# Feed-forward tail of a Mamba-2 block: low-rank part folded into the weight, 1/sigma applied behind the matmul, layer norm begun a step earlier

## What is computed

```python
x = layernorm(x + mixer(x))            # x: 2 x 512 tokens x 512
# mixer: in_proj, causal conv (4 taps), silu, chunked state-space scan over 128 heads
#   (8 groups, chunks of 128 tokens), y * silu(gate), RMS norm per group of 1024 channels, out_proj
h   = einsum('bsd,nrd->nbsr', x, lora_A)              # 8 adapters of rank 16: 128 rows
out = x @ W.T + bias + einsum('nbsr,nor->bso', h, lora_B * (2 * lora_weights))
x = layernorm(x + out)
```

## Time and profile before

| | us |
|---|---|
| median of 3 runs | 1672.47 (1672.35 to 1673.64) |
| profiled execution, whole | 1674.88 |
| its span, first to last instruction | 1673.1 |
| PE busy | 1618.5 (97%) |
| PEld busy | 1294.7 (77%) |
| DVE busy | 1346.7 (80%) |
| ACT busy | 1225.1 (73%) |
| POOL busy | 1026.7 (61%) |
| from 1571.0 (step 2 of the last unit) to the norm_sum behind the last project_out, 1646.2 | 75.2 |
| from there to the last product, 1667.5 | 21.3 |
| from there to the end | 5.6 |

### The profile page before, as it was taken

How to read it: one execution, slowest core, us unless ns; L and a number is a source line. 1 busy time by engine, 2 the same in 40 slices (tenths; PEclk the granted TensorE clock), 3 DMA queues, 4 the chain that set the end, 5 groups by cost and what they waited for, 6 DMA issues and landing times. The chain is left out here.

```text
span 1673.1 us, 26984 instructions
## 1 busy us (share of the span) xinstructions
PE 1618.5 (97%) x9072; PEld 1294.7 (77%) x9072; DVE 1346.7 (80%) x1855; ACT 1225.1 (73%) x2375; POOL 1026.7 (61%) x829
## 2 busy tenths in 40 slices
PE   7799999999999999999999999999999999999898
PEld 6577887778878788787887788777887778877665
DVE  5487798869988699787988689886998779787776
ACT  5777778777768867777877777787677778677742
POOL 4365756565676656666666666656566666666654
PEclk9899999999999999999999999999999999999999
DMA  3655444544454434544444544544444343434511
GB/s 123 195 129 99 117 95 113 110 105 99 96 143 97 114 84 97 128 100 119 79 121 111 105 104 91 136 96 110 95 90 146 94 124 80 106 114 96 134 32 45
DMA packets 236889, 178.67 MB, mean 107 GB/s; under 512 B 16464, under 2 KB 198736, under 8 KB 236368
## 3 DMA queue, kind: packets, MB, share of 16 engines
q1 hardware_dynamic: 235312, 175.72, 43.3%
q10 hardware_dynamic: 1440, 1.22, 0.2%
HBM read 172.17 MB, written 4.72 MB: 106 GB/s over the span
## 5 line engine op out<-in xcount | busy, mean ns | idle before, releaser
L948 POOL TENSOR_TENSOR w_lo<-raw,w_hi 128x512 fp32r<-128x512 f32 x209 | 292.1, 1398 | 309.2 <-ACT w_hi L709 308.1
L494 PE MATMUL proj<-x_hi,w_hi 128*128 128x512 f32 x1160 | 464.3, 400 | 14.7 <-DVE x_lo L1212 6.9
L495 PE MATMUL proj<-x_lo,w_hi 128*128 128x512 f32 x1160 | 454.2, 392 | 0.0
L496 PE MATMUL proj<-x_hi,w_lo 128*128 128x512 f32 x1160 | 453.8, 391 | 0.0
L1099 DVE SCALAR_TENSOR_TENSOR hs<-proj,uch,hs 128x511 f32<-128x511 f32 (+2 forms) x384 | 285.3, 744 | 64.8 <-ACT hs L736 59.6
L791 ACT ACTIVATE decay<-decay,tok 128x128 f32<-128x128 f32 x1024 | 312.4, 391 | 4.8 <-DMA decay<-acum_d 4.8
L1121 DVE TENSOR_TENSOR decay<-decay,cb 128x1024 f32<-128x1024 f32 x128 | 186.8, 1459 | 101.7 <-ACT decay L797 99.1
L1000 POOL TENSOR_TENSOR dh<-dh,eac 128x512 f32<-128x512 f32 x96 | 130.7, 1362 | 222.7 <-DVE eac L1147 222.7
L494 PEld LDWEIGHTS proj<-x_hi,w_hi 128*128 128x128 f32 x1160 | 219.7, 189 | 58.2 <-issue 13.6
L496 PEld LDWEIGHTS proj<-x_hi,w_lo 128*128 128x128 f32 x1160 | 219.1, 189 | 46.2
L495 PEld LDWEIGHTS proj<-x_lo,w_hi 128*128 128x128 f32 x1160 | 219.8, 189 | 41.8
(11 more groups left out here) (121 smaller groups left out, 2762.2 us busy)
## 6 DMA issues: line engine op xcount, KB each, us to landing
decay<-acum_d SPq DMA_DIRECT2D x128, 512.0 KB, 8.9
raw<-w_t SPq DMA_DIRECT2D x209, 256.0 KB, 6.2
eac<-eacum_d SPq DMA_DIRECT2D x192, 128.0 KB, 8.7
wo_raw<-wo_t SPq DMA_DIRECT2D x32, 256.0 KB, 8.6
c_new<-wo_t SPq DMA_DIRECT2D x32, 256.0 KB, 8.2
hs<-x_t SPq DMA_DIRECT2D x8, 256.0 KB, 5.6
acc<-x_tok SPq DMA_DIRECT2D x1, 2048.0 KB, 8.4
out<-acc SPq DMA_DIRECT2D x8, 256.0 KB, 2.0
```

Of the source, the lines that this page charges most:

```text
L494: nc.tensor.matmul(dst[:], w_hi[:, ws, k, :], x_hi[:, k, cols], start=(k == 0), stop=False)
L495: nc.tensor.matmul(dst[:], w_hi[:, ws, k, :], x_lo[:, k, cols], start=False, stop=False)
L496: mm = nc.tensor.matmul(dst[:], w_lo[:, ws, k, :], x_hi[:, k, cols], start=False, stop=(k == KC - 1))
L948: nc.gpsimd.tensor_tensor(w_lo[:, s].rearrange("p a b -> p (a b)"), raw[:, s, :], w_hi[:, s].rearrange("p a b -> p (a b)").bitcast(F32), A ...
```

## The change

- SP issues the five feed-forward loads at the end of unit 0 (step 7), without the wait for gated. lora_a is laid out 128 x 512, not transposed.
- The low-rank part is folded into the weight once: for each of the four k-slices fold_lora(k) computes A_k^T B on TensorE and adds the identity to its k-th 128 columns (the residual), and fold_weight(k) adds this to the weight on VectorE. B is scaled at the end of step 1; folds 0 and 1 stand in step 2 between yoff and p_yd, folds 2 and 3 at its end; VectorE's first two additions stand before g_lo of step 2, the others at its end.
- lora_down, copy_lora, the product with B and add_bias are gone. ffn is four products.
- ScalarE only centres the chunk (centre). The product of the centred chunk is multiplied by 1/sigma, and the bias added, by one three-operand instruction (add_ffn).
- norm_sum, take_var, inv_rms, add_normed and the first layer norm of chunk t are in step t + 1, at the end of each engine's step; scale_off stands behind take_var and add_out.
- The feed-forward steps are by a table: FFN_AT = {3: (0,), 4: (1, 2), 5: (3,), 6: (4,)}, the sums and the second norm SUM_AT = {4: (0,), 5: (1, 2), 6: (3,)}; the rest is behind the loop. The products take banks proj[1] and proj[2] in turn; turn(7) uses p_hid.
- The second norm is one ScalarE pass with scale and shift (shift_of, GpSimd); the last chunk's is on VectorE.

The diff, cut to its core:

```diff
-        FFN_BANK = lambda t: proj[1][:] if t < CPB or t % 2 == 0 else p_st[:]
+        FFN_BANK = lambda t: proj[1 + t % 2][:]
+        TURN_BANK = lambda t: p_hid[:].rearrange("p a b -> p (a b)") if t == CHUNKS - 1 else proj[0][:]
...
-                        if last and (e, c) == (1, 1):
-                            sp.wait_ge(gated, step(GROUPS - 1, 1, 0))
+                        if last and (e, c) == (0, 7):
...
+            def fold_lora(k):
+                if k == 0:
+                    pe.wait_ge(ffn_loaded, 80)
+                    pe.wait_ge(coef_ready, 1)
...
+                wait(pe, w_folded, k - 1)
+                nc.tensor.matmul(FFN_BANK(k), lora_a_sb[:, k * P:(k + 1) * P], lora_b_sb, start=True, stop=False)
+                nc.tensor.matmul(FFN_BANK(k)[:, k * P:(k + 1) * P], ident[:], ident[:], start=False, stop=True).then_inc(lora_ready, 1)
+            def turn(t):
+                pe.wait_ge(centred, t + 1)
+                if t < CHUNKS - 1:
+                    wait(pe, yt_copied, t)
...
+            def ffn(t):
+                pe.wait_ge(w_folded, KC)
+                wait(pe, ffn_sum, t - 1)
+                pe.wait_ge(yt_copied, t + 1)
                 for k in range(KC):
+                    mm = nc.tensor.matmul(FFN_BANK(t), yT(t)[:, k, :], ffn_w_sb[:, k, :], start=(k == 0), stop=(k == KC - 1))
+                mm.then_inc(ffn_out, 1)
...
+                        if ffn_step and c == 2:
+                            fold_lora(0)
+                            fold_lora(1)
...
-                        if ffn_step and c >= 4:
-                            ffn(c - 4)
-                        if ffn_step and c >= 3:
-                            turn(c - 3)
+                        if ffn_step and c in FFN_AT:
+                            turn(FFN_AT[c][0])
+                        if ffn_step and c == 7:
+                            turn(5)
...
                             project_out(g, e, c - 1)
+                            if ffn_step:
+                                norm_sum(g, c - 1, True)
...
+                        if ffn_step and c == 2:
+                            fold_lora(2)
+                            fold_lora(3)
+                        if ffn_step and c in FFN_AT:
+                            for t in FFN_AT[c][1:]:
+                                turn(t)
+                            for t in FFN_AT[c]:
+                                ffn(t)
...
             project_out(G, 1, 7)
             norm_sum(G, 7, True)
+            ffn(5)
             turn(6)
             turn(7)
             ffn(6)
             ffn(7)
...
+                            for t in FFN_AT.get(c, ()):
+                                copy_turned(t)
+                            if c == 7:
+                                copy_turned(5)
+                            for t in SUM_AT.get(c, ()):
+                                normalize(t)
+                            if c >= 1:
+                                centre(c - 1)
...
+            copy_turned(6)
+            centre(7)
+            copy_turned(7)
+            for t in range(4, CHUNKS - 1):
+                normalize(t)
...
+                            for t in SUM_AT.get(c, ()):
+                                rstd_of(1, t)
+                                shift_of(t)
+                            if c >= 1:
+                                inv_rms(g, c - 1)
+                                rstd_of(0, c - 1)
...
             def add_ffn(t):
-                dve.wait_ge(biased, t + 1)
                 dve.wait_ge(ffn_out, t + 1)
-                nc.vector.tensor_tensor(acc[:, t, :], acc[:, t, :], FFN_BANK(t), ALU.add).then_inc(ffn_sum, 1)
+                dve.wait_ge(ln_rstd[0], t + 1)
+                nc.vector.scalar_tensor_tensor(out=acc[:, t, :], in0=FFN_BANK(t), scalar=rstd[:, 0, t:t + 1], in1=bias_sb,
+                                               op0=ALU.mult, op1=ALU.add).then_inc(ffn_sum, 1)
+            def fold_weight(k):
+                dve.wait_ge(lora_ready, k + 1)
+                nc.vector.tensor_tensor(ffn_w_sb[:, k, :], ffn_w_sb[:, k, :], FFN_BANK(k), ALU.add).then_inc(w_folded, 1)
...
+                        if ffn_step and c == 2:
+                            fold_weight(0)
+                            fold_weight(1)
                         dve.wait_ge(ghi_ready, s + 1)
...
+                        if ffn_step and c == 7:
+                            take_var(g, 6)
+                            add_out(g, 6)
+                        if ffn_step:
+                            for t in SUM_AT.get(c, ()):
+                                add_ffn(t)
+                                ln_begin(1, t)
...
+                        if ffn_step and 0 < c < 7:
+                            take_var(g, c - 1)
+                        if e == 1 and c > 0 and not (ffn_step and c == 7):
                             add_out(g, c - 1)
...
+                        if ffn_step and c < 7 and (c + 1) % CPB:
+                            scale_off(g, e, c + 1)
+                        if ffn_step and c > 0:
+                            add_normed(g, c - 1)
+                            ln_begin(0, c - 1)
...
+                        if ffn_step and c == 1:
+                            dve.wait_ge(ffn_loaded, 80)
+                            nc.vector.tensor_scalar(lora_b_sb, lora_b_sb, lw[:], 2.0, ALU.mult, ALU.mult).then_inc(coef_ready, 1)
+                        if ffn_step and c == 2:
+                            fold_weight(2)
+                            fold_weight(3)
```

More of the change, by code:

```diff
@@ L473, in _ @@
             for t in range(CHUNKS):
-                sp.wait_ge(ln_done[1], t + 1)
+                if t < CHUNKS - 1:
+                    sp.wait_ge(normed, t + 1)
+                else:
+                    sp.wait_ge(last_normed, 1)
                 sp.dma_start(out[t], acc[:, t, :]).then_inc(stored, 16)
@@ L544, in project_out, with norm_sum @@
                 mm.then_inc(out_ready, 1)
-            def norm_sum(g, c, last):
+            def norm_sum(g, c, last=False):
                 pe.wait_ge(sqs_ready, step(g, 1, c) + 1)
@@ L643, in body @@
                             front(0, 0, 0)
-                        if e == 1 and c > 1:
-                            norm_sum(g, c - 2, last)
+                        if ffn_step and c == 2:
+                            fold_lora(0)
+                            fold_lora(1)
+                        if e == 1 and c > 1 and not last:
+                            norm_sum(g, c - 2)
                         elif e == 0 and c < 2 and not (g == 0):
-                            norm_sum(g - 1, 6 + c, False)
+                            norm_sum(g - 1, 6 + c)
                         pe.wait_ge(xdt_ready, s + 1)
@@ L675, in body @@
                             project_out(g, e, c - 1)
-                            if last and (e, c) == (1, 7):
-                                norm_sum(g, 6, True)
+                            if ffn_step:
+                                norm_sum(g, c - 1, True)
                         elif e:
@@ L689, in _ @@
             norm_sum(G, 7, True)
-            turn(5)
-            ffn(4)
-            lora_down(5)
+            ffn(5)
             turn(6)
-            ffn(5)
-            lora_down(6)
             turn(7)
             ffn(6)
-            lora_down(7)
             ffn(7)
@@ L936, in _ @@
             groups(body)
-            for t in range(5, CHUNKS):
-                copy_turned(t)
-                copy_lora(t)
+            copy_turned(6)
[3 more added lines that the diff above has]
+                normalize(t)
         @block.gpsimd
@@ L1050, in lagged_rms @@
             def lagged_rms(g, e, c):
-                if e == 1 and c > 1:
+                if e == 1 and c > 1 and g < G:
                     inv_rms(g, c - 2)
@@ L1059, in rstd_of, with shift_of @@
                 pool.wait_ge(ln_stats[w], t + 1)
[L1060 to L1074 removed]
+                nc.gpsimd.tensor_tensor(rstd[:, w, t:t + 1], var_eps[:, w, t:t + 1], minus_half[:], ALU.pow).then_inc(ln_rstd[w], 1)
+            def shift_of(t):
+                pool.wait_ge(ln_rstd[1], t + 1)
+                nc.gpsimd.tensor_tensor(shift[:, t:t + 1], minus_mean[:, 1, t:t + 1], rstd[:, 1, t:t + 1], ALU.mult).then_inc(shift_ready, 1)
+            groups(body)
             inv_rms(G, 7)
             rstd_of(0, 7)
[L1077 to L1082 removed]
+            for t in range(4, CHUNKS - 1):
+                rstd_of(1, t)
+                shift_of(t)
+            rstd_of(1, CHUNKS - 1)
         @block.vector
@@ L1251, in body @@
                             tap(g, tiles[0], 0, 3)
-                        if e == 1 and c == 7:
+                        if e == 1 and c == 7 and not last:
                             take_var(g, 5)
@@ L1262, in body @@
                         nc.vector.tensor_tensor(y[:], p_yd[:], dh[:], ALU.add).then_inc(y_ready, 1)
-                        if e == 1 and 1 < c < 7:
```

(1 more changed line is left out.)

154 lines of the change are left out of this document (36 added, 118 removed).

## The result

The changed kernel takes 1684.46 us (median of four, 1683.29 to 1686.17) where the kernel before takes 1672.80: 1.0061 times as long, 95% interval 1.0049 to 1.0074 (the two medians alone give 1.0070). A second comparison (e8) gave 1.0049 (1.0037 to 1.0062). The forecast was 1677.5, slower, range 1664 to 1684; the direction and the mechanism held, the size was too small: +5.0 forecast, +8 to +10 by the two ratios, +11.7 by these medians.

What follows compares the result with a forecast made beforehand. TensorE was the fullest engine in loop and tail; the change sets one ring through all engines. Loop waits and slow clock +13.4, work +0.3, tail -8.55, end +0.06 sum to +5.2: 1677.5 us, range 1664 to 1684.

Steps and rivals of the forecast that it cites:

- TensorE's work and the tail: TensorE's work net -9.7 us, nothing saved in the loop; tail behind it 12.75 us against 21.3, so -8.55.
- The ring: Last unit's loop: one chain of waits through all engines, about 12.9 us a step, 13.9 in steps 5 and 6.
- The low clock: TensorE's slow restarts behind the waits for the fold, ffn(0) and ffn(3): 2.0, 1.8 and 1.8, together 5.6 us.
- Rival 3: Much slower, 1683: step 6, step 7 and tail waits also lower the clock, or decay load late; chance 0.10.
- From span to time: The difference from the profiled execution (1674.88 us) was added to the median, 1672.47, giving 1677.7.
- The sum with one SBUF operand: VectorE's three-operand sum behind the product doesn't contend with GpSimd: 0.744 us for 0.69, +0.06 at the end.
- the pow: GpSimd's pow of the first norm, ahead of the next step's dh addition: 0.65 us of the ring.
- Same and faster: Two rivals: 1671.9 with no clock fall, chance 0.24; about 1664 with the loop's waits unchanged, chance 0.21.
- rival 1: Same, 1671.9: the loop's waits come but the clock doesn't fall for them, -5.6 us; chance 0.24.
- rival 2: Faster, about 1664: TensorE's lookahead fills the loop's gaps, waits stay at 12.2 us; chance 0.21.
- The loads: Five feed-forward loads leave SP about 1550 instead of 1564.6, delaying step 4's decay load: 0, or +2 us if later still.

Runs made afterwards that it cites:

- e8: The changed kernel measured again without an edit; 1.0049 times the kernel before.
- e7: The kernel before with the fold, ScalarE only centring and 1/sigma and bias applied behind the product, norm two steps behind as before; 0.9936 of the kernel before.
- e4: The changed kernel with GpSimd's pow of the first norm moved from its step's end to behind the next gate; 1.0008 of the kernel before.
- e9: e7 with the five feed-forward loads issued a step earlier; 0.9952 of the kernel before.
- e5: The changed kernel with folds 0 and 1 behind p_yd and the pow behind the next gate; 0.9989 of the kernel before.
- e6: e5 with ScalarE copying the transposed chunk in front of g_hi and the square of the same step; 0.9977 of the kernel before.
- e3: The kernel before with only the low-rank part and residual folded into the weight; norm, turns and ffn in their old steps; 0.9961 of the kernel before.
- e2: The changed kernel with four useless products filling TensorE's wait in front of ffn(0); 1.0068 of the kernel before.
- e10: e9 with ffn(0) to ffn(2) in front of the state update and ffn(4) before the last output projection; 0.9938 of the kernel before.

## Why the prediction was right, and where it was short

- **TensorE's work and the tail**: right. The tail is 12.9 us for 12.75 forecast, with turn(7) waiting 1.30 (1.4), and 5.7 us behind it (5.66):

```profile
1662.93 3.68 PE L600 MATMUL proj<-hs,raw 128*128 128x512 f32 x8
...
1668.84 7.03 PE L600 MATMUL proj<-hs,raw 128*128 128x512 f32 x16
```

- **The ring**: right in its places. Waits forecast and found, in us: fold 4.1 and 3.88, ffn(0) 3.6 and 3.49, turn(2) 0.8 and none, turn(3) 1.0 and 0.81, ffn(3) 3.5 and 4.17, turn(4) 0.9 and 0.81, ffn(4) 1.8 and 1.70, turn(5) 2.3 and 2.30, project_out(7) 1.9 and 1.96. The y of steps 2 to 7 are within 0.6 us of the forecast, measured from y(1). That y(5) came out so closely is in part luck: ffn(0) took 0.95 us longer than forecast, and the wait of turn(2) went in its place.
- **The low clock**: the term that was mis-sized. Forecast were 2.0, 1.8 and 1.8 us. Behind the fold it took 1.6 (3.78 us to p_yd for 2.17), in ffn(0) 2.75, in ffn(3) 1.8, and in project_out(7), where I had none, 1.6 (4.4 us for 2.85). So 7.7 for 5.6; the second trace (e8) gives 7.6. The 71.3 us busy less 7.7 leave 63.6 of work (63.3 forecast), and with 19.7 of waiting that makes the 91 us. Behind y(1) the trace is 7.4 us longer than that of before where the sum had 5.2, and nearly all of the 2.2 are this term. The timed runs are 8 to 12 us slower; what of that lies beyond the 7.4 is not placed. Rival 3 named such falls, though not this place. The Trainium skill, TensorE: Matmul & The Clock Gate, "HAM oscillation", describes kernels whose recurring waits bring the low clock back each time; in this trace four of the seven waits did, and the seven have no length that parts them (below).
- **From span to time**: 1 us of the trace's +8.4 lies ahead of y(1), where the kernels do the same. Nothing in the forecast covered that a single trace is uncertain by some 3 us there.
- **The sum with one SBUF operand**: right. All eight sums add_ffn of the changed kernel take 0.73 to 0.75 us, but they are no test: GpSimd is idle beside them or runs the one-column pow. In e7 one stands wholly beside a dh addition, and neither is slower for it:

```profile
1617.26 0.74 DVE L1173 SCALAR_TENSOR_TENSOR acc<-proj,rstd,hs 128x512 f32<-128x512 f32 x1
```

```profile
1617.14 1.28 POOL L993 TENSOR_TENSOR dh<-dh,eac 128x512 f32<-128x512 f32 x1
```

  Mix, whose operands are all in SBUF, takes 1.21 to 2.03 in the changed kernel. By the Trainium skill, SBUF - State Buffer, "Who interferes with whom", only an instruction that needs the port shared with GpSimd is held up; these traces agree.
- **What the pieces are worth**: the forecast took the pow as 0.65 us of the ring. By e4 its place cost 2 us in front of y(5), y(6) and y(7) each, and some 6 us in all. It had the wait and what is queued behind it in one sentence, but priced the instruction only. The sum was not harmed, since y(5) to y(7) were followed step by step; the ranking of the pieces was.
- **Same and faster**: the clock did fall, as the rows of both long waits had it (rival 1 is out), and TensorE didn't look ahead over a wait (rival 2 is out).
- **The loads**: the forecast had the five take 7 us to issue, so that the decay load would follow at 1557.3. They took 2.6 (1551.30 to 1553.85) and it followed at 1553.90. The decay came 1.8 us late for ScalarE in step 1 (0.2 in e8), g_lo(1) took 1.53 us as before, and no loss shows. y(2) of e9, 10.84 us behind y(1) for e7's 10.83, agrees.

Put together: the fold is worth 6.5 us and 1/sigma behind the product about 2 to 4; the two parts that change the arithmetic are the gain. The rest of the change is a schedule: the norm begun a step earlier, ffn in the step that y, gate and g_hi belong to, and the second norm in one pass. It lost 16.5 us to e7's schedule (116.7 against 100.3 us from y(1)). No run moved the norm alone. Of the 16.5 us, the place of the folds and of the pow account for 9.9 (e5), the copy for up to 3.5 (e6), and 3.1 remain between e6 and e7, which no run divides further. By the ratios it is 19 to 21 us, and of these 7 remain between e6 and e7: the part without a shown cause may be larger than the traces have it.

## What to carry to other kernels

Price a wait in an in-order queue by what stands behind it, not by the instruction that waits: a 0.55 us pow at the end of a step held a ready addition back for 2 us in each of three steps. When work is moved a step earlier to shorten the tail, check that it doesn't join two engines' chains of the same step; against e7, the changed kernel is 3.8 us shorter from y(7) to the end (27.4 for 31.2) and its y(7) comes 20.3 us later. Most of the tail's gain came with the fold alone: from y(7) on e3 has 31.7 us for 38.1. So change the arithmetic first and leave the schedule alone: that gave e7, and no kernel measured here is faster than it.

## What the runs showed of the hardware

The clock's fall doesn't follow the length of one wait. Behind 2.62 us in e5 the next product ran at full speed (3.67 us), and behind 1.94 us a little later the two products took 8.70 for 7.03. 1.96 us brought it down before project_out(7), 1.70 before ffn(4) did not; and at that same project_out(7) a wait of 1.94 us in e2 did not either (2.8 us for the projection, where the changed kernel has 4.4). The clearest pair is the state update of step 6: behind 3.18 us in e3 it takes 2.04 us (its line is shown there), behind 3.17 us in e9 it takes 1.10:

```profile
1618.12 1.10 PE L653 MATMUL p_st<-xd,b_tok 128*128 128x512 f32 x2 [3.17 <-DVE eac L1125]
```

What parts these two no run shows. The changed kernel lost 2.75 us and 1.8 us at ffn(0) and ffn(3) in one trace, and 1.6 and 2.9 in the other. A wait of 2 to 4 us therefore costs up to 2.9 us more than its length, and kernels with several of them scatter: the twelve runs of e4 lie between 1673.3 and 1681.2, the five of e10 between 1662.3 and 1664.4.
